# Causal bias in spare array lines, split scatters and sixteen fixed expert steps in an image encoder block

## The reference

```python
h = h + _L0_attn_ref(_layernorm(h), w_attn, b_attn, w_proj, b_proj)      # causal, 12 heads of 16
x = _layernorm(h)
a = x + attention(rms_norm(x, norm1_w), w_qkv, w_out)    # causal, 12 heads of 64, 3 for keys and values, rope
moe_in = rms_norm(a, norm2_w).reshape(832, 192)
probs = softmax(moe_in @ w_router)                       # 16 experts
vals, idx = top_k(probs, 2); vals = vals / vals.sum()
for e in range(16):
    gate, up = split(moe_in @ w_gate_up[e])              # 192 -> 2 x 384
    out = out + combine[:, e:e + 1] * ((silu(gate) * up) @ w_down[e])    # 384 -> 192
h = h + a + out
```

## Time and profile before

| | |
|---|---|
| time, median of 3 runs | 322.85 us (322.15 to 323.57) |
| profiled execution | 320.91 us |
| its span | 319.1 us |
| TensorE busy | 271.8 us, 85% of the span |
| its weight loads busy | 227.3 us, 71% |
| VectorE busy | 141.4 us, 44% |
| ScalarE busy | 88.3 us, 28% |
| GpSimd busy | 117.2 us, 37% |
| mean granted clock of TensorE | 0.947 |

### The profile page before, as it was taken

The page is one execution under the profiler, slowest core; times in us unless marked ns, Lnnn a source line. Parts: engine busy times, 40 slices in busy tenths (PEclk is TensorE's granted clock), DMA queues, the critical chain, the costliest instruction groups (busy, mean ns, idle before and its releaser), DMA issues.

```text
span 319.1 us, 5739 instructions
## 1 busy us (share of the span) xinstructions
PE 271.8 (85%) x1947; PEld 227.3 (71%) x1947; DVE 141.4 (44%) x347; ACT 88.3 (28%) x232; POOL 117.2 (37%) x128
## 2 busy tenths in 40 slices
PE   0999999999899999898899999405899999999920
PEld 0888789979589878688888888405677777777710
DVE  0153745865635576437667845740022222222214
ACT  1016841025512045421100632000333333333300
POOL 6041022390021660025593006772235523666220
PEclk9999999999999999999999999555999999999985
DMA  7400995018000043000000001791222596222016
GB/s 291 195 2 21 338 368 141 2 39 259 0 7 15 2 115 84 0 22 2 2 0 2 0 2 41 172 329 27 39 41 45 162 289 195 74 64 74 27 47 225
DMA packets 16353, 30.02 MB, mean 94 GB/s; under 512 B 6404, under 2 KB 10628, under 8 KB 15492
## 3 DMA queue, kind: packets, MB, share of 16 engines
q1 hardware_dynamic: 11140, 20.43, 21.5%
q10 hardware_dynamic: 2752, 5.23, 5.2%
q0 software_dynamic: 2432, 3.96, 4.2%
HBM read 25.52 MB, written 4.09 MB: 93 GB/s over the span
## 4 chain that ended last, share of the span: by engine, by line
PE 63%; POOL 10%; issue 9%; DVE 9%; DMA 5%; ACT 2%; POOLq 0%; SPq 0%; DVEq 0%
PE bank L1345 11%; PE bank L1101 8%; PE bank L1238 8%; PE bank L1113 4%; POOL slots L588 4%; PE bank L1298 4%; PE bank L1256 4%; PE bank L1362 4%; PE bank L1150 3%; POOL parts L610 3%; PE bank L1145 2%; DVE experts L816 2%; PE bank L1132 2%; DMA front<-fw 2%; PE bank L1137 2%
## 5 line engine op out<-in xcount | busy, mean ns | idle before, releaser
L1101 PE MATMUL bank<-constants 128*128 128x96 f32 x326 | 42.3, 290 | 16.2 <-DMA slots<-slot_contents,slot_index 16.2
L1101 PEld LDWEIGHTS bank<-constants 128*128 128x128 f32 x326 | 40.9, 205 | 16.9 <-DMA slots<-slot_contents,slot_index 16.4
L1345 PE MATMUL bank<-experts,probs_by_key 96*128 x152 | 52.3, 487 | 0.6 <-ACT probs_by_key L759 0.6
L1345 PEld LDWEIGHTS bank<-experts,probs_by_key 96*128 96x128 f32 x152 | 27.4, 190 | 15.9 <-issue 0.8
L1054 DVE TENSOR_TENSOR probs_by_key<-bank,probs_by_key 128x384 f32<-128x384 f32 x19 | 10.6, 558 | 59.7 <-PE bank L1345 59.7
L604 POOL DMA_INDIRECT front<-moe_in,probs_by_key x21 | 20.1, 957 | 38.0 <-DMA front<-moe_in,probs_by_key 32.7
L1238 PE MATMUL bank<-experts,front 96*96 96x208 f32 x160 | 29.0, 339 | 0.8 <-DVE experts L911 0.8
L1238 PEld LDWEIGHTS bank<-experts,front 96*96 96x96 f32 x160 | 26.0, 163 | 3.1 <-DVE experts L911 1.2
L515 POOL TENSOR_TENSOR rstd_b<-variance_b,constants 128x2 f32<-128x2 f32 x4 | 2.8, 708 | 63.9 <-DVE variance_b L949 63.9
L911 DVE TENSOR_TENSOR experts<-bank,constants 96x416 f32<-96x416 f32 x40 | 21.1, 580 | 10.7 <-POOL experts L563 10.1
L610 POOL DMA_INDIRECT parts<-front,probs_by_key x19 | 18.7, 982 | 14.4 <-DVE front L1058 10.4
(11 more groups left out here) (167 smaller groups left out, 440.1 us busy)
## 6 DMA issues: line engine op xcount, KB each, us to landing
experts<-wgu SPq DMA_DIRECT2D x6, 768.0 KB, 8.8
experts<-wgu SPq DMA_DIRECT2D x12, 288.0 KB, 7.8
patches<-xp SPq DMA_DIRECT2D x6, 384.0 KB, 4.0
experts<-wdn SPq DMA_DIRECT2D x1, 2304.0 KB, 16.7
experts<-wdn ACTq DMA_DIRECT2D x8, 288.0 KB, 5.2
front<-fw SPq DMA_DIRECT2D x1, 1840.0 KB, 10.2
experts<-wgu ACTq DMA_DIRECT2D x4, 288.0 KB, 8.1
front<-fw SPq DMA_DIRECT2D x1, 776.0 KB, 9.0
```

Of the source, the lines that this page charges most:

```text
L1101: mm(bank[:, 0:96], eye, eye[:, 0:96], start=True, stop=True)
L1345: last = mm(ps[2 * half][:, 0:FF], xT[:, 128 * k:128 * k + 128], big[0:C, bass.ds(e * (4 * FF) + (GU0 + 2 * FF * k + FF * half), FF)], sta ...
```

## The change

It has four parts.

1. **Causal bias.** `mask_keys` and its calls go. The operands of the score products are carved over all 128 partitions: in A, `q1_all` and `kbd_all` hold the one-hot table and the mask in their partitions 96 to 127; in B, `qr_all` and `kbd2_all` hold them in partitions 96 to 121 of the first of two halves. So the score products read 128 (or 122) partitions instead of 96 and add the bias themselves. ScalarE writes these partitions by copies from the constants: at its start for both buffers of A, in b1 of groups 0 and 3 for those of B. The filler counts change: 5 to 9 in a4(0), and 20, 20, 4, 17 to 14, 14, 4, 15 in b4.
2. **Scatters.** The first six of sixteen are queued on POOL behind phase 5 of B2, ahead of POOL's b6(2); two follow where eight stood, and eight at the end.
3. **Fixed steps.** Every expert gets one unconditional step, in the order of the experts, with weights at constant addresses; only further tiles (`LISTED` = 12 at most) run under a condition with registers. SP loads the entries of the sixteen first tiles in four transfers without reading the list. Late weights have a semaphore for each expert. VectorE's lists cover only the extra tiles. In a conditional step the register with the expert for `down` is read ahead of the turns.
4. **128 and 64 channels.** The 192 channels are split 128 + 64 instead of 96 + 96. `wgu` holds, for each expert, 2 x 384 columns for the first 128 channels and 384 columns in which the last 64 channels of gate stand in partitions 0 to 63 and those of up in 64 to 127. `copy_x` becomes three copies: the first 128 channels, and the last 64 once to each half of the partitions, into columns of their own with zeros opposite (a memset by POOL). In a fixed step, `gate_and_up` first makes the two products of 64 partitions, one on the upper and one on the lower half of the array, then two of 128 partitions. In an extra step all four are of 128 partitions.

```diff
-LISTED = SLOT_TILES + 5
+LISTED = STEPS - E
+KNOWN = ((0, 1), (1, 2), (2, 9), (9, E))
...
+            for n, (a, b) in enumerate(KNOWN):
+                sp.dma_start(entry[:, 3 * a:3 * b].rearrange("p (e n) -> p e n", n=3),
+                             by_expert[:, a:b, 0, :]).then_inc(known_in[n], 16)
             sp.wait_ge(eid_ready, 1)
-            for j in range(STEPS):
-                place = sp.value_load(ei[0:1, 2 * LISTED + j:2 * LISTED + j + 1], min_val=0, max_val=E * MOST)
-                sp.dma_start(entry[:, 3 * j:3 * j + 3], slots[bass.ds(place * 128, 128), :]).then_inc(entry_in[j], 16)
+            for n in range(LISTED):
+                j = E + n
+                place = sp.value_load(ei[0:1, 2 * LISTED + n:2 * LISTED + n + 1], min_val=0, max_val=E * MOST)
+                sp.dma_start(entry[:, 3 * j:3 * j + 3], slots[bass.ds(place * 128, 128), :]).then_inc(extra_in[n], 16)
...
-                   [b1, b2, nothing, nothing, nothing, b6, nothing, nothing], {7: scatter})
-            scatter(1)
+                   [b1, b2, nothing, nothing, nothing, b6, nothing, nothing], {5: lambda q: scatter(q, range(3)), 7: lambda q: scatter(q, range(3, RT))})
+            pool.wait_ge(pv2_done, 9)
+            pool.memset(xT[:, 128:384], 0.0).then_inc(x_zeros, 1)
+            scatter(1, range(RT, TILES))
...
-            pool.wait_ge(eid_ready, 1)
-            used = tiles_used(pool)
...
+            gather(0)
+            for j in range(1, AHEAD):
+                gather_ahead(j)
+            pool.wait_ge(eid_ready, 1)
+            used = tiles_used(pool)
...
+            act.wait_ge(first_in, 16)
+            act.wait_ge(consts_in, 16)
+            for g in range(2):
+                act.activation(A[g].q1_all[C:128].rearrange("p c (i q) -> p (c i) q", q=32),
+                               eye[C:128, C:128].unsqueeze(1).to_broadcast([32, 2 * GI, 32]), ACT.Copy)
+                act.activation(A[g].kbd_all[C:128].rearrange("p c i h k -> p (c i h) k"),
+                               mask1[C:128].unsqueeze(1).to_broadcast([32, 2 * GI * HC, S]), ACT.Copy).then_inc(mask_a, 1)
+
+            def mask_rows(w):
+                act.activation(w.qr_all[C:C + S, 0].rearrange("p i r q -> p (i r) q"),
+                               eye[C:C + S, C:C + S].unsqueeze(1).to_broadcast([S, GI * R, S]), ACT.Copy)
+                act.activation(w.kbd2_all[C:C + S, 0].rearrange("p i g k -> p (i g) k"),
+                               mask1[C:C + S].unsqueeze(1).to_broadcast([S, GI * G, S]), ACT.Copy).then_inc(mask_b, 1)
...
             def copy_x(j):
                 act.wait_ge(xtr_done, j + 1)
-                act.activation(xT, ps[6][0:C, 0:256], ACT.Copy).then_inc(xT_ready, 1)
+                act.activation(xT[:, 0:128], ps[6][:, 0:128], ACT.Copy)
+                for half in range(2):
+                    last = act.activation(xT[64 * half:64 * half + 64, 128 + 128 * half:256 + 128 * half],
+                                          ps[6][0:64, 128:256], ACT.Copy)
+                last.then_inc(xT_ready, 1)
...
                 if g == 0:
-                    pe.wait_ge(consts_in, 16)
-                    keep_busy(w.ps[1], 5)
-                for t in range(GT):
-                    for i in range(IPT):
-                        mask_keys(w.ps[1 + t], slice(32 * i, 32 * i + 32), eye[0:32, 0:32], (0, 32 * i))
+                    keep_busy(w.ps[1], 9)
...
-                                      w.q1[:, c, 128 * t + 32 * i:128 * t + 32 * i + 32],
-                                      w.kbd[:, c, IPT * t + i].rearrange("p h k -> p (h k)"), start=False, stop=(c == 1),
+                                      w.q1_all[:, c, 128 * t + 32 * i:128 * t + 32 * i + 32],
+                                      w.kbd_all[:, c, IPT * t + i].rearrange("p h k -> p (h k)"), start=True, stop=True,
...
-                for t in range(GT):
-                    mask_keys(w.ps[t], slice(0, 104), const("same_query", S), None)
...
-                keep_busy(w.ps[3], (20, 20, 4, 17)[g])
+                keep_busy(w.ps[3], (14, 14, 4, 15)[g])
...
             def x_turn(j):
                 pe.wait_ge(gathered, j * 16 + 16)
-                for c in range(2):
-                    last = pe.transpose(ps[6][0:C, 128 * c:128 * c + 128], xy[:, j * D + C * c:j * D + C * c + C], eye)
-                last.then_inc(xtr_done, 1)
+                pe.transpose(ps[6][:, 0:128], xy[:, j * D:j * D + 128], eye)
+                pe.transpose(ps[6][0:64, 128:256], xy[:, j * D + 128:j * D + D], eye).then_inc(xtr_done, 1)
...
+            def gate_and_up(j, e):
+                if j < E:
+                    a = GU0 + (E - 1 - j) * 3 * FF
+                    for half in range(2):
+                        rows = slice(64 * half, 64 * half + 64)
+                        mm(ps[2 * half][:, 0:FF], xT[rows, 128 + 128 * half:256 + 128 * half],
+                           big[rows, a + 2 * FF:a + 3 * FF], start=True, stop=False, tile_position=(64 * half, 0))
+                    for half, done in enumerate((gate_done, up_done)):
+                        mm(ps[2 * half][:, 0:FF], xT[:, 0:128], big[:, a + FF * half:a + FF * half + FF],
+                           start=False, stop=True).then_inc(done, 1)
+                else:
+                    for half, done in enumerate((gate_done, up_done)):
+                        mm(ps[2 * half][:, 0:FF], xT[:, 128 + 128 * half:256 + 128 * half],
+                           big[:, bass.ds(e * (3 * FF) + (GU0 + 2 * FF), FF)], start=True, stop=False)
+                        mm(ps[2 * half][:, 0:FF], xT[:, 0:128], big[:, bass.ds(e * (3 * FF) + (GU0 + FF * half), FF)],
+                           start=False, stop=True).then_inc(done, 1)
...
             pe.wait_ge(scattered, 16 * TOPK * TILES)
             keep_busy(ps[7], 16)
-            pe.wait_ge(eid_ready, 1)
-            used = tiles_used(pe)
             x_turn(0)
             pe.wait_ge(early_in, 16 * 7)
-            step(0, prior=False)
-            step(1, first=True)
-            for j in range(2, FEWEST):
-                step(j)
+            for j in range(E):
+                step(j)
+            pe.wait_ge(eid_ready, 1)
+            used = tiles_used(pe)
```

More of the change, by code:

```diff
@@ L75 @@
 NFRONT = _n
-GU0 = E * 3 * D
+SPARE = 8 * FF
+GU0 = E * 3 * D + SPARE
 class Buffers:
@@ L585, in scatter @@
                 pool.wait_ge(idx_ready, q + 1)
-                for t in range(RT * q, RT * q + RT):
+                for t in ts:
                     for k in range(TOPK):
@@ L752, in _ @@
             act.wait_ge(tokens_out[1], 2 * 16 * IPT)
-            load_late(act, 0, LATE_PARTS * 3 // 2)
+            for n in range(LATE // 2):
+                load_late(act, n)
             act.wait_ge(eid_ready, 1)
@@ L772, in step @@
                 copy_x(j + 1)
+            act.wait_ge(x_zeros, 1)
             copy_x(0)
```

173 lines of the change are left out of this document (86 added, 87 removed).

## The result

The changed kernel takes 318.65 us (median of 4 runs, 317.53 to 319.01), the kernel before, beside it, 322.88: ratio 0.985, 95% interval 0.982 to 0.988. It is faster by 1.5%, outside the 0.5% that a measurement can tell. I had forecast 322.6 us and no change; the range, 315.8 to 326.5, holds the time, the likeliest case was not the one that came.

A forecast was written before the change was run, and what follows sets the result against it. TensorE's stream without holes was taken to bound the expert loop, POOL's scatters the way there. Masks -3.5, scatters +1.3, first step +0.35, fixed steps +0.6, extra steps +1.0: -0.25 us, so 322.6 from 322.85; range 315.8 to 326.5.

The forecast's parts named there:

- The expert steps: Gate and up in the expert loop: pair saves 0.645 us, tile changes cost 0.68; +0.6 us over sixteen fixed steps.
- the 64-column half of the new x_turn: Small turn in each expert step, forecast to pay two changes of tile, at 0.17 us each.
- The price of one: One change between whole array and tile in the expert steps, taken at 0.17 us, or 0.13 for leaving a tile.
- the extra steps: The three remaining expert steps keep 2.58 us of gate and up and pay two changes of tile: +1.0 us.
- rival (a): Expert steps: the 64-column turn costs no change of tile, -6.5 us over 19 steps, 316.1 us; chance 0.22.
- The causal bias: Attention without mask products: 0 in the first pair, 1.27 us each in second and third, 0.98 in last; 3.5 won.
- Rival (b): TensorE's clock falls behind the late rstd before about 197 us: +2 to 4 us, about 325.5 us; chance 0.18.
- The scatters: Six scatters on POOL ahead of b6(2) make rstd 2.8 us late and the last scatter 1.3 us later.
- Rival (d): POOL's six early scatters end in time: -1.3 us instead of +1.3, 320.0 us; chance 0.13.
- The first step: First step of the expert loop: copy_x as three copies is not hidden there, +0.35 us.

## Why the prediction was right in its range and wrong in its likeliest case

**The expert steps: the step that failed.** "So the 64-column half of the new x_turn should pay as well." It doesn't: L1365, L1366 and L1400 follow each other at 0.11 us. I had read the 0.17 us of L1150, whose operands have 26 lines, as the price of any product smaller than the array. It told nothing of a turn of 128 lines and 64 columns, and the nearer row, small columns on all lines without a position, wasn't there. A fixed step has two changes of tile, not four, an extra step none. The price of one was too low: 0.20 us, taken at 0.17 and 0.13. The 0.13 of the earlier trace rows goes only to the start of L1298, and the 0.11 behind that start, which the same trace has, isn't in it. So 0.40 instead of 0.68 a step, -0.25 instead of +0.04 net, -4.0 us instead of +0.6 over sixteen, and 0 instead of +1.0 for the extra steps. This is rival (a), given 0.22, with a worse price: it said 3.8 us a step. By these starts the pair overlaps fully, as taken. The estimate from the Trainium skill's 3.07 times (TensorE: Matmul & The Clock Gate, Measured speedup vs the span model), 0.84 us for the pair, is what the rows show from its start to that of the full products. The rows point to another reason than a poor overlap, though: another 0.09 and 0.11 us stand outside the pair, and the whole array behind column tiles shows the same 0.11. The Trainium skill's rule on the drain (TensorEngine Tiling (Array Packing), Key Properties), which I set against rival (a), agrees with the pair, which pays, and says nothing against the turn: the rows show no change of mode there.

**The causal bias.** Right: 0 in the first pair (first exponential at 37.92 for 37.83), 1.43 us in the second and in the third, taken at 1.27 each; with the last, 3.96 by the slot numbers where the clock holds, taken at 3.5. What was missed is the work that the masks did unread: they filled the hole ahead of b3(3). I had written that b3(3) can't start before the rope sums, and not asked what TensorE does until then. Rival (b) named the clock, but behind rstd, before about 197 us, or at the fillers of b4. It falls there as well, in the first profile to 0.50 from 198 to 200, so the rival came true in part: its price there is 0.9 us, not 2 to 4. The larger price, 2.46 us, was paid at 170, in some executions and not in others.

**The scatters.** Right in mechanism: rstd directly behind the sixth, the second slot numbers late, by 2.7 to 3.7 us counted from the first ones (22.11 and 23.03 us, for 19.37), taken as 2.6. The size was too small: the first of the six starts 0.97 us after the slot numbers are ready, which the row of before with its wait at another place didn't show, so rstd is about 3.6 us late instead of 2.8; the clock behind it adds 0.9 in most profiles. The stretch to the last scatter is 1.7 to 2.9 us longer instead of 1.3. Rival (d) falls.

**Costed at nothing, and not nothing.** The late weights' new packing is in no term. The last scatter lands 1.05 to 1.6 us sooner in the changed kernel. The run with the weights moved shows that they were what delayed it in the kernel before; that it is their packing over 128 partitions that frees the queues sooner is only argued (smaller pieces left it at 2.15). It fits that from 212 to 216 us the DMA engines are fully busy in both kernels and move 238 to 247 GB/s before, 392 to 414 in the changed one. The gathers: in the first profile one is late for 1.26 us. The first step costs 0.38 us more from x_turn to the pair, taken as 0.35.

**The sum.** For the first profile, between landmarks, changed minus before: +0.1 to the first exponential, -1.5 attention, +2.9 scatters, -1.05 landing, -0.2 to the first h_turn, -2.5 steps (-3.8, and 1.3 for the gather), +0.2 at the end: -2.0, the difference of the spans. For the second profiles of both: +0.5, -4.0, +1.7, -1.6, +0.5, -3.8, +1.5: -5.2, again the difference of the spans. The medians, 4.2 and 4.9 us apart, lie between, as executions with and without the fall do. That the range held is in part luck. Gains that the sum didn't have, about 5.6 us on the steps (forecast +1.6, measured -4.0) and 1.05 to 1.6 at the landing, met costs that it didn't have either: 2.46 for the clock at 170, 0.4 to 1.6 at the scatters and up to 1.3 for a gather.

## What to carry to other kernels

A product that is removed may have been doing a second job: ask of every instruction taken out of the busiest engine what fills its place until the next one can start. Work put early into an in-order queue must fit into the gap ahead of the next critical entry: two scatters fit here, six cost 1.7 to 2.6 us. For products side by side count the changes of tile, at about 0.20 us each here, and read the price past the first product behind the change, not only up to its start; two half-height products of 384 columns repay two changes, by 0.25 us.

## What the runs showed of the hardware that was not expected

- A turn of 128 lines and 64 columns that names no tile position goes between whole-array products at 0.11 us, like one of 128 columns.
- A change of tile costs about 0.20 us, and not all of it ahead of the first product behind it: about 0.10 us are lost before that product's start and 0.11 between it and its successor, into the row tiles, out of them, and out of the column tiles of the kernel before.
- Behind a hole of 1.2 us in TensorE's work the clock fell to half in three profiles of five, at a price of 2.46 us, and in two it didn't. Behind the wait for a late rstd it fell in five of six, at 0.9 us.
- Small transfers that land beside late weights take 1.3 to 1.6 us longer (from the last scatter's start to TensorE's wake, 3.4 to 3.7 us against 2.2), and a gather 5.9 us where others take 2.9.
